# First stage: statistics and rows between the links of the chains, a tile of every group on GpSimd

## The reference

```
xn = (x - mean) / sqrt(var + 1e-5)                 # per token
# linear attention, 16 heads of 8, per sequence
q, k = elu(xn @ Wq.T) + 1, elu(xn @ Wk.T) + 1;  v = xn @ Wv.T
kv = sum_n k v^T;  den = q . sum_n k
att = ((q kv) / (den + 1e-6)) @ Wo.T
# one expert of 8 per token
aff = xn @ centroids.T;  e = argmax(aff);  alpha = sigmoid(aff[e])
h  = layernorm(xn, g[e], b[e], eps=1e-5)           # a second norm of xn
ye = xn + relu(h @ w1[e].T + b1[e]) @ w2[e].T + b2[e]
out = x + att + alpha * ye + (1 - alpha) * xn
```

## Time and profile before

| | us |
|---|---|
| median of 3 runs | 167.02 (166.9 to 167.08) |
| profiled execution | 168.04 |
| its span, first to last instruction | 166.3 |

### The profile page before, as it was taken

How to read it: one execution, slowest core, us unless ns; L and a number is a source line. 1 busy time by engine, 2 the same in 40 slices (tenths; PEclk the granted TensorE clock), 3 DMA queues, 4 the chain that set the end, 5 groups by cost and what they waited for, 6 DMA issues and landing times.

```text
span 166.3 us, 4561 instructions
## 1 busy us (share of the span) xinstructions
PE 139.1 (84%) x1106; PEld 130.8 (79%) x1106; DVE 109.6 (66%) x387; ACT 105.8 (64%) x332; POOL 117.8 (71%) x132
## 2 busy tenths in 40 slices
PE   0056969799979999999999999799599999999810
PEld 0055969698967888898999999798499999999700
DVE  3899494999976888897565653545467665565410
ACT  8477898899455676675666666654666666655500
POOL 7600000499868898889888768787887888888883
PEclk9999999999999999999999999999999999999995
DMA  4999000293007953343358858766598778634433
GB/s 146 306 367 384 4 0 0 80 340 107 4 16 235 312 193 108 102 106 100 98 171 258 278 166 181 172 121 174 117 162 171 173 170 178 106 35 45 39 32 32
DMA packets 19113, 24.05 MB, mean 145 GB/s; under 512 B 2576, under 2 KB 13328, under 8 KB 18960
## 3 DMA queue, kind: packets, MB, share of 16 engines
q1 hardware_dynamic: 13456, 19.50, 36.4%
q0 software_dynamic: 5632, 4.26, 18.8%
HBM read 17.40 MB, written 6.36 MB: 143 GB/s over the span
## 4 chain that ended last, share of the span: by engine, by line
PE 46%; POOL 18%; DVE 18%; issue 9%; ACT 4%; DMA 2%; DVEq 2%; ACTq 0%
POOL out L358 18%; PE bank L610 11%; PE bank L622 10%; PE bank L575 5%; PE bank L592 4%; PE bank L565 3%; PE bank L583 3%; PE bank L511 3%; PE bank L502 3%; DVE lane_neg L809 2%; DMA x<-in_x 2%; DVE stats L672 2%; PE bank L602 2%; DVE kv_all L857 1%; ACT xn L397 1%
## 5 line engine op out<-in xcount | busy, mean ns | idle before, releaser
L466 ACT ACTIVATE hT<-bank,b 128x128 f32<-128x128 f32 x156 | 44.6, 370 | 27.5 <-PE bank L610 22.7
L358 POOL DMA_INDIRECT out<-rows,token_at x32 | 50.1, 1565 | 11.2 <-issue 7.9
L622 PE MATMUL bank<-w,hT 128*128 x312 | 42.9, 281 | 4.1 <-ACT hT L466 3.6
L622 PEld LDWEIGHTS bank<-w,hT 128*128 128x128 f32 x312 | 37.8, 191 | 6.0 <-issue 5.6
L610 PE MATMUL bank<-zT,feat_k 128*128 128x128 f32 x312 | 41.3, 275 | 0.0
L610 PEld LDWEIGHTS bank<-zT,feat_k 128*128 128x128 f32 x312 | 37.9, 192 | 0.0
L345 POOL DMA_INDIRECT rows<-z_rows,token_at x32 | 32.3, 1009 | 6.5 <-issue 6.5
L366 POOL TENSOR_TENSOR feat_k<-feat_k,k_exp 128x256 f32<-128x256 f32 x16 | 14.4, 920 | 26.0 <-ACT k_exp L445 25.5
L910 DVE TENSOR_SCALAR zT<-xn,ln_g,ln_b 128x128 f32 x39 | 14.6, 376 | 9.4 <-issue 9.3
L923 DVE SCALAR_TENSOR_TENSOR rows<-y_own,weight,rows 128x128 f32 x39 | 13.7, 352 | 7.6 <-DVE y_own L917 5.0
L915 DVE TENSOR_TENSOR weight<-own,rows 128x1 f32<-128x1 f32 x39 | 6.6, 169 | 17.5 <-PE bank L622 13.7
(11 more groups left out here) (112 smaller groups left out, 229.5 us busy)
## 6 DMA issues: line engine op xcount, KB each, us to landing
feat_k<-in_w1T SPq DMA_DIRECT2D x39, 256.0 KB
z_rows<-xn SPq DMA_DIRECT2D x4, 528.0 KB, 5.8
w<-in_w2T SPq DMA_DIRECT2D x1, 2048.0 KB, 9.7
out<-x SPq DMA_DIRECT2D x8, 256.0 KB
x<-in_x SPq DMA_DIRECT2D x2, 768.0 KB, 7.1
x<-in_x SPq DMA_DIRECT2D x2, 256.0 KB, 2.8
b<-in_b SPq DMA_DIRECT2D x1, 512.0 KB, 5.2
rows<-z_rows,token_at POOLq DMA_INDIRECT x32
```

What stands on the lines that cost most here:

```text
L358: g.indirect_dma_start(out=out_rows, out_offset=bass.IndirectOffsetOnAxis(ap=token_at[:, t:t + 1], axis=0), in_=rows[:, t, 0:D], in_offset ...
L466: last = a.activation(hT[:, par, c * P:(c + 1) * P], bank[hidden_bank(s)][:, c * P:(c + 1) * P], ACT.Relu, bias=b1[:, c, bass.ds(e, 1)])
L622: last = t_.matmul(bank[y_bank(s)][:, 0:D], hT[:, par, c * P:(c + 1) * P], w2[:, bass.ds(e * (FC * D) + c * D, D)], start=(c == 0), stop=( ...
```

## The change

x is loaded in eight transfers of four tiles, and the loads of centroids and Wv are issued by ScalarE, at its very start. `statistics` is one sequence over all 32 tiles, and every chain takes fillers from it: chunk 0 the nine tiles behind it, chunk 1 nine more (`FILLED`), and the chain of chunk 2 takes rows of chunk 1. Only the first variance is in the chain. EPS is added inside ScalarE's root (a bias), the Newton step is written with `var_half` in three operations behind the reciprocal, and `shift` is gone. The second variance is one operation over all tiles; its root is taken on ScalarE in one piece behind `sqrt_of(2)`, which has moved from behind the copy of group 3 to behind that of group 2, and the rest of it is in `second_norm`, which now stands behind the first part of `choose`. Rows are normalised by VectorE (the first three of each group) and GpSimd (the fourth); ScalarE does none. Its expansion of lanes is cut in four pieces. Nothing behind the first stage is changed.

```diff
-    X_FIRST = 4
+    XG = 4
-    XN_ACT = (3, 2, 1)
+    XN_POOL = 1
+    FILLED = 9
+    LANE_PARTS = 4
...
-            load_x(0, X_FIRST).then_inc(x_first_in, 16)
-            for c in range(NCH):
-                load_x(X_FIRST if c == 0 else CHUNK[c], CHUNK[c + 1]).then_inc(x_in[c], 16)
-            sp.dma_start(cent_wv[:, 0:E], cent_dram).then_inc(cent_wv_in, 16)
-            sp.dma_start(cent_wv[:, E:E + D], wv_dram).then_inc(cent_wv_in, 16)
+            for i in range(NT // XG):
+                load_x(i * XG, (i + 1) * XG).then_inc(x_in[i], 16)
...
+            g.memset(eps_ln[:, :], EPS_LN).then_inc(eps_ready, 1)
...
+            def normalise(gr):
+                pool.wait_ge(rstd_ready, chunk_of(gr * TG) + 1)
+                for t in range((gr + 1) * TG - XN_POOL, (gr + 1) * TG):
+                    last = g.tensor_scalar(xn[:, t, 0:D], x[:, t, :], mean[:, t:t + 1], rstd[:, t:t + 1], ALU.subtract, ALU.mult)
+                last.then_inc(xn_by_pool, 1)
+            for gr in range(NG):
+                normalise(gr)
...
-                a.activation(std[:, :, part], var_e[:, :, part], ACT.Sqrt).then_inc(std_ready, 1)
+                a.activation(std[:, part], var[:, part], ACT.Sqrt, bias=eps_ln[:, 0:1]).then_inc(std_ready, 1)
+            def sqrt_of_second():
+                act.wait_ge(var_2_ready, 1)
+                a.activation(std_2[:, :], var_2[:, :], ACT.Sqrt).then_inc(std_2_ready, 1)
...
+            act.dma_start(cent_wv[:, 0:E], cent_dram).then_inc(cent_wv_in, 16)
+            act.dma_start(cent_wv[:, E:E + D], wv_dram).then_inc(cent_wv_in, 16)
             act.wait_ge(rows_ready, 1)
             a.activation(warm[:, :], lane_row[:, 0:1], ACT.Sqrt)
-            expand_lanes()
+            expand_lanes(0)
+            act.wait_ge(eps_ready, 1)
             sqrt_of(0)
-            normalise(0)
-            normalise(1)
+            expand_lanes(1)
+            expand_lanes(2)
             copy_xnT(0)
             copy_xnT(1)
             sqrt_of(1)
             copy_v(0)
             copy_v(1)
-            normalise(2)
-            normalise(3)
+            expand_lanes(3)
             for gr in range(2, NG + LAG):
                 if gr < NG:
                     copy_xnT(gr)
-                if gr == 3:
+                if gr == 2:
                     sqrt_of(2)
+                    sqrt_of_second()
                     a.activation(warm[:, :], mean[:, 0:1], ACT.Exp, scale=0.0)
-                if gr + 2 < NG:
-                    normalise(gr + 2)
...
-                step(v_.scalar_tensor_tensor(var, ms_a[:, 2, 0:n], 1.0 / D, ms_b[:, 0, 0:n], ALU.mult, ALU.add), filling)
-
-                v_.tensor_scalar(var_e[:, 0, part], var, 1.0, EPS_LN, ALU.mult, ALU.add)
-                v_.tensor_scalar(var_e[:, 1, part], var, 1.0 + EPS_LN, EPS_LN * EPS_LN, ALU.mult, ALU.add).then_inc(var_ready, 1)
+                v_.scalar_tensor_tensor(var[:, part], ms_a[:, 2, 0:n], 1.0 / D, ms_b[:, 0:n], ALU.mult, ALU.add).then_inc(var_ready, 1)
...
             def rsqrts(c, filling):
+                next(filling, None)
+                next(filling, None)
+                dve.wait_ge(var_ready, c + 1)
+                v_.tensor_scalar(var_half[:, part], var[:, part], -0.5, -0.5 * EPS_LN, ALU.mult, ALU.add)
+                next(filling, None)
                 dve.wait_ge(std_ready, c + 1)
-                dve.wait_ge(var_ready, c + 1)
-                step(v_.reciprocal(rinv[:, :, 0:n], std[:, :, part]), filling)
-                step(v_.tensor_tensor(nw_a[:, :, 0:n], rinv[:, :, 0:n], rinv[:, :, 0:n], ALU.mult), filling)
-                step(v_.tensor_tensor(nw_b[:, :, 0:n], nw_a[:, :, 0:n], var_e[:, :, part], ALU.mult), filling)
-                step(v_.tensor_scalar(nw_a[:, :, 0:n], nw_b[:, :, 0:n], -0.5, 1.5, ALU.mult, ALU.add), filling)
-                step(v_.tensor_tensor(rstd[:, :, part], rinv[:, :, 0:n], nw_a[:, :, 0:n], ALU.mult), filling)
-                v_.scalar_tensor_tensor(shift[:, part], mean[:, part], -1.0, rstd[:, 0, part], ALU.mult, ALU.mult).then_inc(rstd_ready, 1)
+                step(v_.reciprocal(rough[:, part], std[:, part]), filling)
+                step(v_.tensor_tensor(nw_a[:, 0:n], rough[:, part], rough[:, part], ALU.mult), filling)
+                step(v_.tensor_tensor(nw_b[:, 0:n], nw_a[:, 0:n], var_half[:, part], ALU.mult), filling)
+                v_.scalar_tensor_tensor(rstd[:, part], nw_b[:, 0:n], 1.5, rough[:, part], ALU.add, ALU.mult).then_inc(rstd_ready, 1)
+                next(filling, None)
+                dve.wait_ge(rstd_ready, c + 1)
...
-            finish(statistics(0))
-            moments(0, nothing)
-            rsqrts(0, nothing)
+            seen = statistics()
+            some(seen, CHUNK[1])
+            moments(0, seen)
+            rsqrts(0, seen)
             finish(normalise(0))
-            finish(statistics(1))
-            filling = statistics(2)
-            moments(1, filling)
-            rsqrts(1, filling)
-            finish(normalise(1))
-            finish(filling)
-            moments(2, nothing)
-            rsqrts(2, nothing)
+            some(seen, CHUNK[2] - CHUNK[1] - FILLED)
+            moments(1, seen)
+            rsqrts(1, seen)
+            rows_1 = normalise(1)
+            some(rows_1, TG - XN_POOL)
+            finish(seen)
+            moments(2, rows_1)
+            next(rows_1)
+            dve.wait_ge(var_ready, NCH)
+            v_.tensor_scalar(var_2[:, :], var[:, :], 1.0 + EPS_LN, EPS_LN * EPS_LN, ALU.mult, ALU.add).then_inc(var_2_ready, 1)
+            rsqrts(2, rows_1)
+            finish(rows_1)
             finish(normalise(2))
...
             def second_norm():
-                v_.tensor_tensor(spread[:, :], var_e[:, 0, :], rstd[:, 0, :], ALU.mult).then_inc(chain, 1)
-                dve.wait_ge(chain, chained[0] + 1)
-                v_.tensor_tensor(xn[:, :, AT_C], spread[:, :], rstd[:, 1, :], ALU.mult).then_inc(meta_ready, 1)
+                dve.wait_ge(var_2_ready, 1)
+                v_.tensor_scalar(var_2_half[:, :], var_2[:, :], -0.5, None, ALU.mult)
+                v_.scalar_tensor_tensor(spread[:, :], var[:, :], EPS_LN, rstd[:, :], ALU.add, ALU.mult)
+                dve.wait_ge(std_2_ready, 1)
+                step(v_.reciprocal(rough_2[:, :], std_2[:, :]), nothing)
+                step(v_.tensor_tensor(sq_2[:, :], rough_2[:, :], rough_2[:, :], ALU.mult), nothing)
+                step(v_.tensor_tensor(nw_2[:, :], sq_2[:, :], var_2_half[:, :], ALU.mult), nothing)
+                step(v_.scalar_tensor_tensor(rstd_2[:, :], nw_2[:, :], 1.5, rough_2[:, :], ALU.add, ALU.mult), nothing)
+                v_.tensor_tensor(xn[:, :, AT_C], spread[:, :], rstd_2[:, :], ALU.mult).then_inc(meta_ready, 1)
...
-            for c in range(len(CHOOSE) - 2):
+            choose(0)
+            second_norm()
+            for c in range(1, len(CHOOSE) - 2):
                 choose(c)
             dve.wait_ge(const_ready, 8)
             v_.tensor_copy(token_half[:, :], token_no[:, :]).then_inc(starts_full, 1)
-            second_norm()
             choose(len(CHOOSE) - 2)
```

More of the change, by code:

```diff
@@ L271, in _ @@
             sp.wait_ge(meta_ready, 2)
-            sp.wait_ge(xn_by_act, NG)
+            sp.wait_ge(xn_by_pool, NG)
             sp.wait_ge(xn_by_dve, NG)
@@ L391, in copy_xnT, with expand_lanes @@
                 a.activation(xnT[:, gr * TG * P:(gr + 1) * TG * P], bank[gr % 2][:, :], ACT.Copy).then_inc(xnT_ready, 1)
-            def normalise(gr):
-                act.wait_ge(rstd_ready, chunk_of(gr * TG) + 1)
-                for t in range(gr * TG, gr * TG + XN_ACT[chunk_of(gr * TG)]):
-                    last = a.activation(xn[:, t, 0:D], x[:, t, :], ACT.Identity, bias=shift[:, t:t + 1], scale=rstd[:, 0, t:t + 1])
-                last.then_inc(xn_by_act, 1)
-            def expand_lanes():
-                act.wait_ge(rows_ready, 1)
-                a.activation(lane_neg[:, :, :], lane_row[:, :].unsqueeze(2).to_broadcast([P, P, NT]), ACT.Copy).then_inc(lane_full, 1)
+            def expand_lanes(q):
+                some = slice(q * P // LANE_PARTS, (q + 1) * P // LANE_PARTS)
+                a.activation(lane_neg[:, some, :], lane_row[:, some].unsqueeze(2).to_broadcast([P, P // LANE_PARTS, NT]), ACT.Copy)\
+                 .then_inc(lane_full, 1)
             def copy_v(b):
@@ L663, in _, with statistics @@
             v_ = nc.vector
-            def statistics(c):
-                if c < NCH:
-                    dve.wait_ge(x_in[c] if c else x_first_in, 16)
-                    for t in range(CHUNK[c], CHUNK[c + 1]):
-                        if t == X_FIRST:
-                            dve.wait_ge(x_in[c], 16)
-                        ins = v_.bn_stats(stats[:, t, :], x[:, t, :])
-                        if t == CHUNK[c + 1] - 1:
-                            ins.then_inc(stat_done, 1)
-                        yield
+            def statistics():
+                for t in range(NT):
+                    if t % XG == 0:
```

(5 more changed lines are left out.)

38 lines of the change are left out of this document (20 added, 18 removed).

## The result

The changed kernel takes 166.19 us (median of 9 runs, 165.29 to 166.36), the kernel before 167.32 in the runs beside it (9, 166.9 to 168.34). The ratio is 0.9916 with a 95% interval of 0.9888 to 0.9943: 0.84% faster. The profiled execution went from 168.04 to 166.33, a gain of 1.71 where 2.5 were forecast. The medians lie 1.13 apart.

The account below looks back on a forecast made before the run. A chain of waits, nearly half TensorE, then GpSimd, passes first-stage gains to the end. 2.3+0.33-0.1 = 2.5 us off 168.04 gives 165.5, median 1.0 lower: 164.5; own range 163.8 to 165.3, wider 163.4 to 166.2.

Parts of the forecast that it names:

- nothing after the ranks is touched by the change: Behind the first stage: work after the ranks stays as it was, so only when `chosen` is ready matters.
- the median of the runs is 1.0 lower: From profiled execution to median: 1.0 us comes off, taking the forecast from 165.5 to 164.5.
- Chunk 0: First chain: reciprocal stays at 7.20, `rstd` at 8.3, TensorE starts at 9.3 instead of 9.93, gain 0.6 us.
- Chunk 1: Second chain: VectorE in time, reciprocal at 12.35, `rstd` at 13.4, transposes of group 2 at 14.4 instead of 15.65.
- Chunk 2: Third chain: table load done with warm-up at 18.1, `copy_v(2)` at 18.5 releases `values(5)`, `values(12)` starts 2.3 us earlier.
- GpSimd's tiles: GpSimd normalises one tile of four at 0.65 us, upper end 1.3; the later ones have cover.
- Second norm: Behind `choose(0)`: some 1.5 us of work lies in VectorE's wait for `choose(1)`, gain 0.33; uncovered it would cost 1.2.
- Loads: Start of the first stage: x for chunk 0's fillers lands just in time; centroids and Wv cost 0.1 us, ends 0 and 1.0.
- Everything behind the ranks moves by the same amount: From the ranks to the end: what the first stage gives goes through microsecond for microsecond, 2.5 us forecast.
- The rows did not exclude each other: Rival: GpSimd's rows stop VectorE's for their length, 167.3 us at 0.6 each, 169.8 at 0.9; chances 0.03 and 0.10.
- The late loads: Rival: chunk 0's fillers wait 1.0 us for one piece of x, giving 165.4; chance 0.12.
- The change did reach TensorE: Rival claimed the opposite: TensorE stays slow until after 20, 2.0 us lost, giving 166.5; chance 0.05.

Follow-up runs that it names:

- delay2: The changed kernel with ten more `bn_stats` (output unused) on VectorE ahead of the last part of `choose`; median 168.12 us, ratio 1.0048.
- norm_late: The changed kernel with 8 unused words behind `warm`, and `second_norm` back in front of the last part of `choose`; median 167.12 us, ratio 0.996.
- best: Changed kernel with late table load, small loads on SyncE, four chunk 0 fillers, ScalarE rows for groups 0 and 1, GpSimd constants behind `rstd`; 165.97 us, ratio 0.9876.
- before: The kernel before the change, nothing altered; median 167.32 us in the runs beside the changed kernel, profiled execution 168.04.
- act_row0: The changed kernel with the fourth row of groups 0 and 1 on ScalarE instead of GpSimd; median 165.47 us, ratio 0.9864.
- few_fill: The changed kernel with 8 unused words behind `warm`, and four statistics instead of nine in chunk 0's chain; median 166.02 us, ratio 0.9885.

## Why the prediction was right or wrong

**Right in direction and in what the first stage does, too large in size.** The median of 166.19 is 1.69 above 164.5: outside the forecast's own range of 163.8 to 165.3, and inside the wider one by 0.01, which is luck. As a gain it is 1.13 where 2.5 were forecast. Two steps failed: "nothing after the ranks is touched by the change", where the runs show 0.35 us, and "the median of the runs is 1.0 lower", where it was 0.14 lower. The rest is mis-sized terms of the first stage, 0.38 at the ranks in the one profile and 0.1 to 0.2 in its repeats (28.4 forecast; 28.78, 28.47, 28.58). In the profiled execution the error is 0.8 (166.33 against 165.5); the other 0.9 came with the step from that execution to the median.

**Chunk 0: mis-sized.** The variance was taken to come "one step earlier" and came at 6.97+0.17, so that the reciprocal stood at 7.71 and not at 7.20: the first load was 0.4 later, which put L704 beside GpSimd's `v_all` memset, where it lasted 0.62, as L701 had in the earlier trace rows (with the small loads behind x it ran at 5.87, in 0.17). That row was in the prediction, and its sum did not carry it over. `rstd` was ready at 8.51+0.15 instead of 8.3. GpSimd's row, priced at 0.65 with an upper end of 1.3, took 0.79 to 1.11. TensorE started at 10.03, not 9.3. Of this 0.7 about 0.3 could have counted, the 0.33 that VectorE waited for the root of chunk 1; it is gone in the repeats that start at 9.89 or 9.90. Beyond it the start does not bind: with a start at 9.53, bought with later statistics, group 2 came later. The forecast's gain of 0.6 in chunk 0 lay for the most part on that edge.

**Chunk 1: mis-sized by 0.66.** But for those 0.33, what binds is VectorE's queue of statistics, moments and chain. The forecast had VectorE "there in time" with its variance at 11.5 for a reciprocal at 12.35, and left out what its own change puts between the two, three statistics and `var_half`, which it had counted in chunk 0 (about 0.8). The variance was ready at 11.84+0.15, and the queue up to the reciprocal ran to 12.66. `rstd` was ready at 13.97 instead of 13.4, the transposes of group 2 at 15.06 instead of 14.4.

**Chunk 2: the right stall, its size right.** The load of 1.28 starts at 17.36 instead of 16.6, and `values(5)` (the half behind it) at 19.29 instead of 18.5: 0.8 late. From there 5.07 to `values(12)` instead of 5.35, so 0.3 came back; 24.36 against 23.85. TensorE's pace was already the quick one at 15.06 (0.66 for four transposes), which the prediction did not expect. It gave nothing, as TensorE waited for the copy anyway: slow or quick behind group 2's start, `values(12)` came 9.27 to 9.30 later in all eight profiles with the load in that place. The load had its place in the prediction as what comes before `copy_v(2)`, "which releases `values(5)`"; that moving it away brings the ranks 1.36 sooner, where the whole change brings 2.17, was not seen.

**GpSimd's tiles: right outside chunk 0.** The later six rows had cover, although they took 0.8 each, not 0.65.

**Second norm: right.** Its 0.33 is the difference between the gains at `values(12)` and at the ranks (2.17-1.84). The chain was priced at 1.5, or 1.2 more than the old one, and measured as 1.35, or 1.0 more.

**Loads: right in the sum, wrong in the place.** The loads of x for the fillers were in time. The two small loads delayed the very first piece by 0.4 instead, and taking them back moved neither the ranks (28.50, within the repeats) nor the time by anything that can be told.

**"Everything behind the ranks moves by the same amount": the first failing step.** As a rule of waits it holds: the delay of 1.73 to 1.93 at the ranks came out as 1.93. But "nothing after the ranks is touched by the change" is false. Its new sizes moved `tile_val` by 480 bytes (inferred from the sizes), that is 32 off a multiple of 64, and the matmuls of `tokens` went from 2.06 to 2.41. That is the 0.35 between the ranks and the gather, of the 0.8 by which the profiled execution missed. The prediction had its own test for this ("if the end isn't 2.5 earlier") and no view of it.

**The step to the median: the second failing step, 0.9.** "The median of the runs is 1.0 lower" took one profiled execution of the kernel before as a constant. It was an execution of the upper group; after the change the profiled one (166.33) is 0.14 above the median. The medians of the kernel before, 167.02 to 168.09 over its sets of runs, lie 1.1 apart, nearly as much as this change gains. The 1.13 between the medians mix the groups too: of the nine runs before, four are in the lower group and four in the upper, of the nine after one and eight. Like with like, the change gives 1.82 in the upper group (168.03 to 166.21) and 1.75 in the lower (167.04 to 165.29, one run), close to the 1.71 of the profiled executions; this split by eye is an estimate. So the difference of like executions is the number to forecast. What makes the two groups is open. A hint: from the first to the last scatter it is 65.82 to 66.01 in some profiled executions (both kernels) and 65.52 to 65.58 in others (only versions of the changed one), with the same work; but `delay2`, with 65.52, was profiled in an upper execution of its own, so this is not all of it, and no experiment was made on it.

**The rivals.** The rows did not exclude each other: VectorE's 24 rows lasted 0.33 to 0.43 beside GpSimd's, which took 0.79 to 1.11 where 0.65 had been taken from L353. The late loads showed only once the two small ones were taken away (0.60 at tile 12). The change did reach TensorE. The Trainium skill, "SBUF — State Buffer" (section "Who interferes with whom"), says that `tensor_scalar` can contend with GpSimd when its operands meet certain conditions, and that whoever comes second then waits in full; the prediction had told it without the condition. The traces agree for the moments beside a memset (0.62) and for a row beside an iota (0.97, seen once), and disagree for the rows beside GpSimd's `tensor_scalar` (0.45 at the most).

## What to carry to other kernels

Price a start that comes sooner by what waits at the next hand-over: here at most 0.3 us of a sooner first matmul could count, while taking one table load of 1.28 us off ScalarE's copies brought the ranks 1.36 sooner. Don't add up gains that were measured apart: a slow pace that a wait had hidden showed as soon as the wait was gone. A change to the tiles' sizes moves every tile behind them: compare operations the change does not touch, and try a few words of padding before reading a difference as schedule. Profile the same stage more than once before reading 0.3 us as an effect. Forecast the ratio or the difference of like executions, and don't carry the distance of one profiled execution to a median as a constant.

## What was not expected of the hardware

- 32 matmuls with f16 operands read with a stride (`tile_val`, `lane_hot`) took 2.00 to 2.16 us in eight profiles and 2.35 to 2.42 in the other six, by where the tiles lay to 32 bytes.
- VectorE's row took 0.33 to 0.45 beside GpSimd's `tensor_scalar` and once 0.97 beside its iota. GpSimd's own row took 0.79 to 1.11 with two pointer scalars and two operations; one pointer and one operation took 0.65.
- Loads of 68 KB on ScalarE's queue delayed the first 256 KB of x on SyncE's by 0.4 us.
- Behind waits of TensorE of 1.94 to 2.52 us the granted clock fell to 0.50 for 3 us and more (`norm_late`, `best`, `delay2`), and the matmuls took up to twice their time. In `before`, `act_row0` and `few_fill` they were as slow behind group 2's start while the granted clock read as full.
